# Last combination of a two-layer attention and expert kernel: three of eight batches on ScalarE and GpSimd

## Chip, cores and metric

The kernel runs on one core of one Trainium2 chip. The metric is the device time of one execution in microseconds; the median of several executions counts.

## What is computed

`x` is 8 batches of 256 tokens with 256 features, float32. Two layers follow each other. Each adds to `x` a gated cross-attention over 120 context rows, and then a gated mixture of 8 experts of which each token uses two. The end of a layer, cut to what matters here, is

```python
x = x + jnp.tanh(g_xattn[l]) * attention_l(_layernorm(x), ctx)
x = x + jnp.tanh(g_ffn[l]) * experts_l(_layernorm(x))
...
sel = jnp.take_along_axis(out_all, top_k_idx[:, :, None], axis=1)
out = jnp.sum(sel * router_probs[:, :, None], axis=1)
```

So for each token the outputs of its two experts are multiplied by the token's two weights (with tanh of the gate in them) and added to `x`. This weighted sum, for the second layer, is the combination that the change touches.

## The kernel before

The five engines run programs of their own and meet at semaphores (`wait_ge`, `then_inc`). All of `x` stays on the chip as `x_sb`, 128 partitions x 16 tiles x 256: batch b is the tiles 2b and 2b + 1.

In each layer the attention and the routing run over 16 tiles. During them GpSimd computes the layer norm's reciprocal deviations in tiny operations (L458 to L463) and scatters normalised tokens to a buffer in device memory, sorted by expert (L488); ScalarE applies the norm (L558, L601: 128x256, scale and bias read from the chip's memory). Then the experts run over 39 blocks of 128 tokens: SyncE loads a block (L374), TensorE multiplies (L1302, L1329), ScalarE and VectorE copy and activate, and GpSimd scatters each block's result to its tokens' rows of `ys_dram` (L494).

When all blocks are stored, SyncE (waiting at L391) issues eight loads, one for each batch, of 512 KB into `yg` (L393): `yg[:, b, t, k, :]` is the output of choice k for tile t of batch b. Load b counts up the semaphore `D_gl[b]`. The function `combine(L, b)` of VectorE (L744 to L754) waits for that load and then issues four instructions at L753, for k = 0, 1 and t = 0, 1:

```python
v.scalar_tensor_tensor(out=xt, in0=yg[:, b, t, k, :], scalar=wcomb[:, 2 * b + t, k:k + 1],
                       in1=xt, op0=ALU.mult, op1=ALU.add)
```

The second of a tile waits for the first (`d_c1`), and each second one counts up `d_comb`. The weights `wcomb` are computed on VectorE just before the expert blocks (L1005 to L1015, semaphore `C_v`). The combination of layer 0 is spread over the attention of layer 1 (the same L753, from 522 to 632 us); that of layer 1 stands at the very end of VectorE's program, batches 0 to 7 one after another. SyncE goes through the batches in the same order: it waits for `d_comb`, issues the store of batch b, 256 KB from `x_sb` to `out` (L399), and in the end waits for all stores (L401). Loads and stores are all issued from SyncE, on one hardware queue, the loads first. During this tail ScalarE, TensorE and GpSimd have nothing to do; ScalarE's last work is a copy at L678 at 807.5 us, GpSimd's the last scatter.

Of the kernel before, what the change touches and what calls it, by code (L numbers as in the profile page):

```python
# [19 lines left out]
ALU = mybir.AluOpType  # L20
ACT = mybir.ActivationFunctionType
# [12 lines left out]
def apart(eng, passed, *waits):  # L34


    for sem, v in waits:
        need(eng, sem, v)
    if any(not isinstance(v, int) for _, v in waits):
        eng.sem_inc(passed, 1)  # L40


def flamingo_kernel(nc, x, ctx_rows, mask, g_xattn, g_ffn, attn_w, attn_b, router_w, experts, out):
    NB, S, D = x.shape
# [5 lines left out]
    NT = NB * S // P  # L50
# [4 lines left out]
    TOPK = 2  # L55
# [15 lines left out]
    with es:  # L71
        def sb(name, shape, dt=F32):
            return es.enter_context(nc.sbuf_tensor(name, shape, dt))

        def sem(name):
            return es.enter_context(nc.semaphore(name))


        x_sb = sb("x_sb", [P, NT, D])
# [46 lines left out]
        yg = w_all[:, NE * EW[1]:NE * EW[1] + NB * QT * TOPK * D].rearrange("p (b t k d) -> p b t k d", b=NB, t=QT, k=TOPK)  # L126
# [43 lines left out]
        wcomb = sb("wcomb", [P, NT, TOPK])  # L170
# [33 lines left out]
        D_gl = [sem(f"results_loaded{b}") for b in range(NB)]  # L204
# [5 lines left out]
        C_v = sem("consts_vector")  # L210
# [32 lines left out]
        d_comb, d_c1 = (sem(n) for n in ("combined", "combine_step"))  # L243
# [6 lines left out]
        b_x, b_up, b_h, b_hT, b_y = (sem(n) for n in ("blkT_psum", "up_psum", "h_used", "hT_psum", "y_psum"))  # L250
        e_x, e_act, e_hT, e_hTv, e_y, e_h = (sem(n) for n in ("blkT_ready", "act_ready", "hT_ready_a", "hT_ready_v", "y_ready", "h_ready"))
        g_z = sem("zeros_ready")
        d_bo = sem("bias_rows_step")
        g_id = sem("token_numbers_ready")
        g_pass = sem("results_passed")
# [12 lines left out]
            return v_early[0:K, b, :, :, :] if b < 2 else v_late[0:K, b - 2, :, :, :]  # L268

        FILL_V = {0: 2, 1: 3, 4: 4, 5: 5, 6: 6, 7: 7}  # L270

        def at(u):
            return u // 2, u % 2 == 0, u // 2 + 1 < NB

        def run_blocks(eng, l, step):


            for j in range(U3 + 1):
                step(j, j % U3, (j - 1) // U3, j == 0, False)
            with eng.Fori(1, (MAX_BLOCKS - U3) // U3) as i:  # L280
                for u in range(U3):
                    step(U3 * i + (1 + u), (1 + u) % U3, i, False, False)
            for j in (MAX_BLOCKS - 2, MAX_BLOCKS - 1):
                step(j, j % U3, (j - 1) // U3, False, j == MAX_BLOCKS - 1)
# [26 lines left out]
        def _(sp):  # L311
# [83 lines left out]
                                     "(t p k) d -> p t (k d)", t=QT, k=TOPK)).then_inc(D_gl[b], 16)  # L395
            ov = out.rearrange("b (t p) d -> p b t d", p=P)
            for b in range(NB):
                sp.wait_ge(d_comb, NT + 2 * (b + 1))
                sp.dma_start(ov[:, b, :, :], x_sb[:, 2 * b:2 * b + 2, :]).then_inc(D_out[b % 2], 16)  # L399
            sp.wait_ge(D_out[0], 16 * NB // 2)  # L400
            sp.wait_ge(D_out[1], 16 * NB // 2)  # L401
# [3 lines left out]
        def _(g):  # L405
# [31 lines left out]
            def late_consts():  # L437

                g.memset(tri[:], 1.0).then_inc(C_g, 1)
                g.memset(lower[:], 1.0).then_inc(C_g, 1)  # L440
                g.wait_ge(C_g, 15)

                g.affine_select(out=tri[:], in_=tri[:], compare_op=ALU.is_ge, fill=0.0, base=-1,
                                pattern=[[1, P]], channel_multiplier=-1).then_inc(C_g, 1)

                g.affine_select(out=lower[:], in_=lower[:], compare_op=ALU.is_ge, fill=0.0, base=-1,
                                pattern=[[1, NE], [-1, NE]], channel_multiplier=0).then_inc(C_g, 1)
                ramp(iota8[:], NE, 1, 0, 0).then_inc(C_g, 1)
                ramp(eR[:], NE, REGION, 0, 0).then_inc(C_g, 1)
                ramp(thr[:], NT, P, 0, 0).then_inc(C_g, 1)  # L450
                ramp(jrow[:], MAX_BLOCKS, 1, 0, 0).then_inc(C_g, 1)
                ramp(tokid[:], NT, TOPK * P, 0, TOPK).then_inc(C_g, 1)
                ramp(spare[:], MAX_BLOCKS, P, NT * P * TOPK, 1).then_inc(C_g, 1)
                g.wait_ge(C_g, 23)
# [10 lines left out]
            def ln1_rstd(B):  # L465
                f = B % 2
                g.wait_ge(d_mv1, 2 * B + 2)
                need(g, a_xn1, B - 1)
                rstd((mv1[:, f, :, 0], mv1[:, f, :, 1]), ve1[:, f, :], rstd1[:, f, :], nm1[:, f, :], mhalf[:],
                     g_ve1, g_pw1, B + 1, g_rs1)  # L470

            def ln2_rstd(G):
                qt = G % 2
                g.wait_ge(d_mv2, G + 1)
                need(g, a_xn2, G - 1)
                rstd((mv2[:, qt, 0:1], mv2[:, qt, 1:2]), ve2[:, qt:qt + 1], rstd2[:, qt:qt + 1], nm2[:, qt:qt + 1],
                     mhalf[:, 0:1], g_ve2, g_pw2, G + 1, g_rs2)

            def scatter(B):
                l, b = B // NB, B % NB  # L480
                s = (NU * l + 2 * b) % 6
                g.wait_ge(d_e0, B + 1)
                g.tensor_copy(xn2[:, s:s + 2, D], tokid[:, 2 * b:2 * b + 2]).then_inc(g_id, 1)
                g.wait_ge(g_id, B + 1)
                g.wait_ge(d_slot, B + 1)
                for t in range(2):
                    for k in range(TOPK):
                        g.indirect_dma_start(xs_dram, bass.IndirectOffsetOnAxis(ap=slot_now[:, B % 2, t, k:k + 1], axis=0),  # L488
                                             xn2[:, s + t, :], None).then_inc(D_sc[B % 2], 16)

            def store_block(l, j, u):
                J = MAX_BLOCKS * l + j
                apart(g, g_pass, (e_y, J + 1), (d_dest, J + 1))
                g.indirect_dma_start(ys_dram, bass.IndirectOffsetOnAxis(ap=dest_i[:, u:u + 1], axis=0),  # L494
                                     y_sb[:, u, :], None).then_inc(D_y[u], 16)

            for l in range(2):
                if l == 1:
                    g.memset(v_late[:, :, :, 1, :], 1.0).then_inc(C_vz, 1)
                ln1_rstd(NB * l)  # L500
                ln1_rstd(NB * l + 1)
                if l == 0:
                    late_consts()
                for u in range(NU):
                    b, even, nxt = at(u)
                    B, G = NB * l + b, NU * l + u
                    if even:
                        if b >= 3:
                            scatter(B - 3)
                    elif b + 2 < NB:  # L510
                        ln1_rstd(B + 2)
                    if u > 0:
                        ln2_rstd(G - 1)
                scatter(NB * l + NB - 3)
                ln2_rstd(NU * l + NU - 1)
                for h in range(2):
                    g.wait_ge(p_pv[h], NU * (l + 1))
                g.memset(zrow, 0.0).then_inc(g_z, 1)
                g.wait_ge(g_z, 2 * l + 1)
                g.memset(zrow[:, D:D + 1], 1000000.0).then_inc(g_z, 1)  # L520
                scatter(NB * l + NB - 2)
                scatter(NB * l + NB - 1)
                for j in range(U3):
                    store_block(l, j, j)
                with g.Fori(1, MAX_BLOCKS // U3) as i:
                    for u in range(U3):
                        store_block(l, U3 * i + u, u)


        @block.scalar  # L530
        def _(a):
# [9 lines left out]
            for l in range(2):  # L541
# [136 lines left out]
                    a.copy(hT[:, 0:n, :], ps[:, 4, 0:n * P].rearrange("p (c n) -> p c n", c=n)).then_inc(e_hT, 1)  # L678
                run_blocks(a, l, blk)


        @block.vector
        def _(v):
# [47 lines left out]
            for l in range(2):  # L731
# [13 lines left out]
                def combine(L, b):  # L745

                    v.wait_ge(D_gl[b], 16 * (L + 1))
                    for k in range(TOPK):
                        for t in range(2):
                            if k:  # L750
                                v.wait_ge(d_c1, 2 * (NB * L + b) + t + 1)
                            xt = x_sb[:, 2 * b + t, :]
                            v.scalar_tensor_tensor(out=xt, in0=yg[:, b, t, k, :], scalar=wcomb[:, 2 * b + t, k:k + 1],  # L753
                                                   in1=xt, op0=ALU.mult, op1=ALU.add).then_inc(d_comb if k else d_c1, 1)  # L754
# [125 lines left out]
                for u in range(NU):  # L880
                    b, even, nxt = at(u)
# [17 lines left out]
                    divide(G)  # L899
                    if l == 0 and u in FILL_V:  # L900
                        values(B0 + FILL_V[u], 5)
                logits_copy(G0 + NU - 3, 5)
# [115 lines left out]
                run_blocks(v, l, blk)  # L1018

            for b in range(NB):  # L1020
                combine(1, b)


        @block.tensor
        def _(t):
            t.wait_ge(C_id, 2)

            for l in range(2):
# [178 lines left out]
                for u in range(NU):  # L1207
# [18 lines left out]
                    if l == 0 and u == 0:  # L1226
                        t.wait_ge(a_ctx, 4)
                        t.wait_ge(d_v, 2)
                    if l == 0 and u - 1 in FILL_V:
                        t.wait_ge(d_v, FILL_V[u - 1] + 1)  # L1230
                    if l == 0 and u - 1 in (2, 3):
# [22 lines left out]
                    if u >= 2:  # L1254
                        x2_t(G - 2)
                    if l == 0 and u in FILL_V:
                        v_proj(B0 + FILL_V[u], 5)
                    if l == 0 and u in (2, 3):
# [135 lines left out]
```

## Time and profile before

| | us |
|---|---|
| median of 3 runs | 833.12 |
| the three runs | 834.97, 833.12, 832.74 |
| the profiled execution, its own time | 834.21 |
| the profiled execution, span from first to last instruction | 832.4 |

The span leaves 1.8 us of the profiled execution's own time around it. The profile counts instructions by engine (PE is TensorE, PEld its weight loads, DVE is VectorE, ACT ScalarE, POOL GpSimd, SP SyncE; a q behind a name is that engine's queue of instructions or DMAs), by line of the kernel (L753 is line 753) and by shape. All times in it are microseconds from the span's start unless ns is said. In a row of a group, "busy, mean ns of one | idle" are the summed busy time, the mean duration, and the idle time of the engine just before. "To landing" of a DMA is from its issue to the last byte's arrival. The last 22 us of the span are the tail of which this case speaks.

### The profile page before, as it was taken

To read this page: it belongs to the slowest core of one execution; us is meant where nothing else is said; L and a number is where in the kernel's file an instruction comes from. 1 tells how busy PE (TensorE), PEld (TensorE's weight loads), DVE (VectorE), ACT (ScalarE), POOL (GpSimd) and SP (SyncE) were. 2 spreads that over 40 slices of the span, in tenths; PEclk is the share of its full clock that TensorE was granted. 3 is DMA by queue.
4 is the path that set the end of the run, shared out by engine and by line. 5 is a ranking of instruction groups with operands and counts; after the bars stand their busy time and mean duration, and the time that the engine had idled before them with its cause. 6 is when DMAs were issued, how large, how long until landed. Compare 5 with 4: busy or idle time off the path is not lost.

```text
span 832.4 us, 19644 instructions
## 1 busy us (share of the span) xinstructions
PE 713.5 (86%) x6306; PEld 538.1 (65%) x6307; DVE 412.3 (50%) x1352; ACT 259.6 (31%) x489; POOL 212.2 (25%) x384
## 2 busy tenths in 40 slices
PE   4899999618999999999999999589899834999980
PEld 3668778506777777777777776477777722666650
DVE  4667787632233322323332332458888752444446
ACT  3555565311111112111111212156555420222220
POOL 4023444540110101011010101112445460333330
PEclk9999999857999999999999999879999965999995
DMA  8044446635111111111110102300112212333328
GB/s 215 9 170 127 161 130 183 200 111 149 32 32 32 38 30 33 32 32 32 32 38 27 36 13 85 137 27 28 54 59 79 97 70 90 93 99 99 93 74 309
DMA packets 50831, 70.41 MB, mean 85 GB/s; under 512 B 7687, under 2 KB 38023, under 8 KB 50771
## 3 DMA queue, kind: packets, MB, share of 16 engines
q1 hardware_dynamic: 42380, 50.85, 20.3%
q0 software_dynamic: 6816, 18.69, 6.4%
q8 instruction: 40, 0.66, 0.3%
q10 hardware_dynamic: 1575, 0.05, 0.2%
q14 instruction: 20, 0.16, 0.1%
HBM read 46.55 MB, written 23.02 MB: 84 GB/s over the span
## 4 chain that ended last, share of the span: by engine, by line
PE 72%; DVE 13%; issue 6%; POOL 3%; ACT 2%; SPq 2%; DMA 2%; DVEq 0%; POOLq 0%; ACTq 0%
PE ps L1302 27%; PE ps L1329 17%; PE ps L1319 5%; PE ps L1123 4%; PE ps L1090 3%; DVE x_sb L753 2%; PE ps L1288 2%; PE ps L1095 2%; PE ps L1062 2%; PE ps L1136 2%; DVE m L768 2%; PE ps L1040 2%; PE ps L1079 2%; DVE ctx_q L777 2%; PE ps L1115 1%
## 5 line engine op out<-in xcount | busy, mean ns | idle before, releaser
L1302 PE MATMUL ps<-w_all,share 128*128 x780 | 236.0, 450 | 3.2 <-DVE share L993 1.6
L1302 PEld LDWEIGHTS ps<-w_all,share 128*128 128x128 f32 x780 | 144.9, 194 | 69.3 <-issue 13.5
L494 POOL DMA_INDIRECT ys_dram<-share,dest_i x78 | 75.1, 963 | 382.6 <-DVE share L1000 374.2
L1329 PE MATMUL ps<-w_all,share 112*128 (+1 forms) x624 | 149.9, 383 | 1.3 <-DVE share L983 0.7
L1329 PEld LDWEIGHTS ps<-w_all,share 112*128 112x128 f32 (+1 forms) x624 | 113.1, 191 | 16.0 <-issue 1.7
L968 DVE TENSOR_TENSOR share<-share,ps 128x344 f32<-128x344 f32 x78 | 40.0, 513 | 145.7 <-PE ps L1302 136.2
L678 ACT COPY share<-ps 128x512 f32<-128x512 f32 (+1 forms) x78 | 37.5, 480 | 200.7 <-PE ps L1319 200.7
L768 DVE TENSOR_REDUCE m<-ps 128x8 f32<-128x960 f32 x64 | 70.3, 1138 | 11.1 <-PE ps L1079 11.0
L670 ACT ACTIVATE share<-ps 128x344 f32<-128x344 f32 x78 | 35.8, 459 | 117.9 <-PE ps L1302 117.9
L488 POOL DMA_INDIRECT xs_dram<-xn,slot_now x64 | 64.7, 1011 | 21.3 <-issue 14.6
L1000 DVE COPY share<-ps 128x256 f32<-128x256 f32 x78 | 33.0, 423 | 72.7 <-PE ps L1329 72.7
L458 POOL TENSOR_SCALAR nm<-mv 128x1 f32<-128x1 f32 (+1 forms) x48 | 11.6, 241 | 182.5 <-DVE mv L802 122.0
L1288 PE MATMUL ps<-ident,share 128*128 128x128 f32 x156 | 31.1, 282 | 31.2 <-DMA share<-xs_dram 30.9
L1288 PEld LDWEIGHTS ps<-ident,share 128*128 128x128 f32 x156 | 21.4, 145 | 48.0 <-issue 36.0
L1319 PE MATMUL ps<-ident,share 128*128 128x128 f32 (+1 forms) x312 | 49.2, 280 | 1.3 <-DVE share L973 0.5
L1090 PE MATMUL ps<-q_flat,w_all 32*120 32x256 f32 x512 | 42.7, 399 | 8.2 <-DVE ctx_q L777 6.0
L1319 PEld LDWEIGHTS ps<-ident,share 128*128 128x128 f32 (+1 forms) x312 | 36.0, 141 | 18.0 <-DVE share L973 8.3
L591 ACT ACTIVATE share<-ps,mask_col 120x1024 f32<-120x1024 f32 x32 | 33.9, 1111 | 37.5 <-PE ps L1095 37.5
L973 DVE TENSOR_TENSOR share<-share 128x256 f32<-128x256 f32 x39 | 16.6, 426 | 57.7 <-ACT share L674 57.7
L1095 PEld LDWEIGHTS ps<-share,sel 32*120 32x120 f32 x1024 | 42.6, 187 | 1.8
L1095 PE MATMUL ps<-share,sel 32*120 32x128 f32 x1024 | 42.0, 277 | 0.0
L1079 PE MATMUL ps<-w_all,q_flat 32*128 32x120 f32 x1024 | 36.5, 280 | 4.0 <-ACT q_flat L573 2.9
(165 smaller groups left out, 949.0 us busy)
## 6 DMA issues: line engine op xcount, KB each, us to landing
share<-xs_dram SPq DMA_DIRECT2D x78, 129.0 KB, 2.1
w_all<-ys_dram SPq DMA_DIRECT2D x16, 512.0 KB, 7.2
w_all<-gate SPq DMA_DIRECT2D x8, 688.0 KB
w_all<-up SPq DMA_DIRECT2D x8, 688.0 KB
w_all<-down SPq DMA_DIRECT2D x8, 560.0 KB
w_all<-w SPq DMA_DIRECT2D x16, 256.0 KB
xs_dram<-share SPq DMA_DIRECT2D x17, 129.0 KB, 2.3
out<-x_sb SPq DMA_DIRECT2D x8, 256.0 KB, 5.1
```

Source lines behind the costliest of these rows:

```text
L488: g.indirect_dma_start(xs_dram, bass.IndirectOffsetOnAxis(ap=slot_now[:, B % 2, t, k:k + 1], axis=0), xn2[:, s + t, :], None).then_inc(D_s ...
L494: g.indirect_dma_start(ys_dram, bass.IndirectOffsetOnAxis(ap=dest_i[:, u:u + 1], axis=0), y_sb[:, u, :], None).then_inc(D_y[u], 16)
L678: a.copy(hT[:, 0:n, :], ps[:, 4, 0:n * P].rearrange("p (c n) -> p c n", c=n)).then_inc(e_hT, 1)
L768: v.tensor_reduce(m4[:, :].rearrange("p (g r) -> p g r", r=Q4)[:, 2 * h:2 * h + 2, 0:4], ps[:, 2 * h:2 * h + 2, 0:4 * K].rearrange("p g (j ...
L968: v.tensor_tensor(h_sb[:, 344 * q:344 * q + 344], act_sb[:, 344 * q:344 * q + 344], ps[:, 2 * q + 1, 0:344], ALU.mult).then_inc(e_h, 1)
L1079: i = t.matmul(ps[:, g, j * K:(j + 1) * K], qT[rows, f, j // 2, j % 2, qt * P:(qt + 1) * P], kT_all[rows, b, j // 2, :], start=(l == 1), s ...
L1090: t.matmul(ps[0:K, 4 + g, 2 * m * P:2 * (m + 1) * P].rearrange("p (e q) -> p e q", e=2), kT_all[rows, b, m, :], qT[rows, f, m, :, qt * P:( ...
L1095: i = t.matmul(ps[0:K, 4 + g, j * P:(j + 1) * P], sel[rows, j, :], mT[rows, :], start=False, stop=(j % 2 == 1))
L1288: i = t.transpose(ps[:, 7, k * P:(k + 1) * P], xg[:, u, k * P:(k + 1) * P], ident[:, :])
L1302: i = t.matmul(ps[:, bank, 0:w], xgT[:, k, :], w_all[:, bass.ds(off + (k * UPW[l] + col - EW[l]), w)], start=(k == 0), stop=(k == KT - 1))
L1319: i = t.transpose(ps[0:n, 4 + c // 4, (c % 4) * P:(c % 4 + 1) * P], h_sb[:, at_:at_ + n], ident[:, :])
L1329: i = t.matmul(ps[:, 6, 0:D], hT[0:r, c, :], w_all[0:r, bass.ds(off + (KT * UPW[l] + c * D - EW[l]), D)], start=(c == 0), stop=(c == KD[l] ...
```

## The change

The last combination of batches 1, 4 and 7 leaves VectorE. For each of them ScalarE waits for the load, and multiplies the four tiles of `yg` by their weights in place (an activation with Identity and the weight as scale); after both tiles of a k it counts up `a_w`. GpSimd, at the end of its program, waits for `a_w` and adds each product to `x_sb` with a `tensor_tensor`; the second of a tile waits for the first. VectorE combines batches 0, 2, 3, 5 and 6 as before. SyncE's loop over the stores stays in batch order, and waits for `g_comb` (GpSimd) or `d_comb` (VectorE) by batch. The combination of layer 0 isn't changed.

```diff
--- before.py
+++ after.py
@@ -250,6 +250,9 @@
         b_x, b_up, b_h, b_hT, b_y = (sem(n) for n in ("blkT_psum", "up_psum", "h_used", "hT_psum", "y_psum"))
         e_x, e_act, e_hT, e_hTv, e_y, e_h = (sem(n) for n in ("blkT_ready", "act_ready", "hT_ready_a", "hT_ready_v", "y_ready", "h_ready"))
         g_z = sem("zeros_ready")
+        g_c1 = sem("combine_step_pool")
+        a_w = sem("results_weighted")
+        g_comb = sem("combined_pool")
         d_bo = sem("bias_rows_step")
         g_id = sem("token_numbers_ready")
         g_pass = sem("results_passed")
@@ -268,6 +271,8 @@
             return v_early[0:K, b, :, :, :] if b < 2 else v_late[0:K, b - 2, :, :, :]
 
         FILL_V = {0: 2, 1: 3, 4: 4, 5: 5, 6: 6, 7: 7}
+
+        POOL_BATCHES = (1, 4, 7)
 
         def at(u):
             return u // 2, u % 2 == 0, u // 2 + 1 < NB
@@ -395,7 +400,10 @@
                                      "(t p k) d -> p t (k d)", t=QT, k=TOPK)).then_inc(D_gl[b], 16)
             ov = out.rearrange("b (t p) d -> p b t d", p=P)
             for b in range(NB):
-                sp.wait_ge(d_comb, NT + 2 * (b + 1))
+                if b in POOL_BATCHES:
+                    sp.wait_ge(g_comb, 2 * (POOL_BATCHES.index(b) + 1))
+                else:
+                    sp.wait_ge(d_comb, NT + 2 * len([n for n in range(b + 1) if n not in POOL_BATCHES]))
                 sp.dma_start(ov[:, b, :, :], x_sb[:, 2 * b:2 * b + 2, :]).then_inc(D_out[b % 2], 16)
             sp.wait_ge(D_out[0], 16 * NB // 2)
             sp.wait_ge(D_out[1], 16 * NB // 2)
@@ -525,6 +533,15 @@
                 with g.Fori(1, MAX_BLOCKS // U3) as i:
                     for u in range(U3):
                         store_block(l, U3 * i + u, u)
+
+            for n, b in enumerate(POOL_BATCHES):
+                for k in range(TOPK):
+                    g.wait_ge(a_w, 2 * n + k + 1)
+                    for t in range(2):
+                        if k:
+                            g.wait_ge(g_c1, 2 * n + t + 1)
+                        xt = x_sb[:, 2 * b + t, :]
+                        g.tensor_tensor(xt, xt, yg[:, b, t, k, :], ALU.add).then_inc(g_comb if k else g_c1, 1)
 
 
         @block.scalar
@@ -678,6 +695,14 @@
                     a.copy(hT[:, 0:n, :], ps[:, 4, 0:n * P].rearrange("p (c n) -> p c n", c=n)).then_inc(e_hT, 1)
                 run_blocks(a, l, blk)
 
+            a.wait_ge(C_v, 2 + 6 * 2)
+            for b in POOL_BATCHES:
+                a.wait_ge(D_gl[b], 32)
+                for k in range(TOPK):
+                    for t in range(2):
+                        i = a.activation(yg[:, b, t, k, :], yg[:, b, t, k, :], ACT.Identity, scale=wcomb[:, 2 * b + t, k:k + 1])
+                    i.then_inc(a_w, 1)
+
 
         @block.vector
         def _(v):
@@ -745,10 +770,11 @@
                 def combine(L, b):
 
                     v.wait_ge(D_gl[b], 16 * (L + 1))
+                    before = NB * L + (b if L == 0 else len([n for n in range(b) if n not in POOL_BATCHES]))
                     for k in range(TOPK):
                         for t in range(2):
                             if k:
-                                v.wait_ge(d_c1, 2 * (NB * L + b) + t + 1)
+                                v.wait_ge(d_c1, 2 * before + t + 1)
                             xt = x_sb[:, 2 * b + t, :]
                             v.scalar_tensor_tensor(out=xt, in0=yg[:, b, t, k, :], scalar=wcomb[:, 2 * b + t, k:k + 1],
                                                    in1=xt, op0=ALU.mult, op1=ALU.add).then_inc(d_comb if k else d_c1, 1)
@@ -1018,7 +1044,8 @@
                 run_blocks(v, l, blk)
 
             for b in range(NB):
-                combine(1, b)
+                if b not in POOL_BATCHES:
+                    combine(1, b)
 
 
         @block.tensor
```

## Rows read from the trace of the kernel before

**Rows 1.** The page, its first table: busy time and share of each engine
```profile
PE 713.5 (86%) x6306; PEld 538.1 (65%) x6307; DVE 412.3 (50%) x1352; ACT 259.6 (31%) x489; POOL 212.2 (25%) x384
```

**Rows 2.** The chain of waits, 780 to 833 us: start, duration, what
```profile
810.46 2.39 DMA ys_dram<-share,dest_i
...
812.92 4.09 DMA w_all<-ys_dram
...
817.04 12.36 DVE x_sb L753 x31
```

**Rows 3.** The timeline, 790 to 833 us: start, duration, engine, line, operation, count
```profile
812.92 4.27 SPq L393 DMA_DIRECT2D w_all<-ys_dram  x8
817.04 12.76 DVE L753 SCALAR_TENSOR_TENSOR x_sb<-w_all,wcomb,x_sb 128x256 f32<-128x256 f32 x32 [7.40 <-DMA w_all<-ys_dram]
818.74 11.46 SPq L399 DMA_DIRECT2D out<-x_sb  x8
```

**Rows 4.** L393, the loads 0 and 1, then 6 and 7: issue and landing
```profile
L393 SPq DMA_DIRECT2D w_all<-ys_dram x2: 387/425/463, 812.9 to 813.4; - x2
...
DMA to landing us min/median/max: 4.1/4.6/5.0
...
L393 SPq DMA_DIRECT2D w_all<-ys_dram x2: 472/522/572, 816.1 to 816.6; - x2
...
DMA to landing us min/median/max: 9.1/9.4/9.8
```

**Rows 5.** L399, the stores 0 and 7: issue and landing
```profile
L399 SPq DMA_DIRECT2D out<-x_sb x1: 383/383/383, 818.7 to 818.7; - x1
...
DMA to landing us min/median/max: 8.4/8.4/8.4
...
L399 SPq DMA_DIRECT2D out<-x_sb x1: 372/372/372, 829.8 to 829.8; - x1
...
DMA to landing us min/median/max: 2.1/2.1/2.1
```

**Rows 6.** Two stretches of the tail, and the queue's total from 805 us
```profile
core 0: us, PE busy (x) PEld busy (x) DVE busy (x) ACT busy (x) POOL busy (x), PEclk, DMA share, GB/s
817.00:820.00 3.00, 0.00 (x0) 0.00 (x0) 2.96 (x8) 0.00 (x0) 0.00 (x0) 0.50 1.04 398
...
826.00:829.00 3.00, 0.00 (x0) 0.00 (x0) 3.00 (x9) 0.00 (x0) 0.00 (x0) 0.50 1.09 383
...
q1 hardware_dynamic: 4352, 6.29, 62.7%
```

**Rows 7.** DMA rate in 40 slices of 0.175 us from 826 us
```profile
GB/s 386 375 386 375 404 380 380 381 386 386 380 381 375 398 380 392 386 375 380 386 380 386 386 375 345 287 182 304 334 357 351 123 0 0 0 0 0 0 0 0
```

**Rows 8.** ScalarE: groups by line and shape, and one pair in the timeline
```profile
L558 ACT ACTIVATE share<-x_sb,nm,rstd 128x256 f32<-128x256 f32 x32 | 17.5, 594 | 18.0 <-POOL nm L463 17.8
...
L558 ACT ACT_TABLE_LOAD x1 | 1.3, 1283 | 8.1 <-POOL nm L463 8.1
...
634.74 1.09 ACT L558 ACTIVATE share<-x_sb,nm,rstd 128x256 f32<-128x256 f32 x2 [1.13 <-POOL nm L463]
```

**Rows 9.** GpSimd: groups by line and shape
```profile
L463 POOL TENSOR_TENSOR nm<-nm,rstd 128x1 f32<-128x1 f32 x32 | 6.1, 192 | 2.5
...
L418 POOL TENSOR_SCALAR_AFFINE_SELECT sel<-sel 128x480 f32<-128x480 f32 x1 | 0.6, 600 | 0.0
...
L412 POOL TENSOR_SCALAR_AFFINE_SELECT ident<-ident 128x128 f32<-128x128 f32 x1 | 0.3, 285 | 0.1
```

**Rows 10.** The timeline of GpSimd near 581 and 676 us
```profile
581.16 0.45 POOL L458 TENSOR_SCALAR nm<-mv 128x1 f32<-128x1 f32 x1 [5.04 <-DVE mv L802]
581.69 0.31 POOL L459 TENSOR_SCALAR ve<-mv 128x1 f32<-128x1 f32 x1
...
675.91 0.24 POOL L458 TENSOR_SCALAR nm<-mv 128x1 f32<-128x1 f32 x1
```

**Rows 11.** The timeline of VectorE near 581 us
```profile
581.05 1.67 DVE L753 SCALAR_TENSOR_TENSOR x_sb<-w_all,wcomb,x_sb 128x256 f32<-128x256 f32 x4
```


## Prediction, made before the changed kernel ran

> **What bounds the kernel now.** The page's first table [rows 1] shows TensorE busy for 86% of the span, but the change touches only the end, so I read the end. The chain of waits [rows 2] says what the last 22 us consist of: the scatter of the last block (2.4 us), the load of the experts' results (4.1 us), then 12.4 us of VectorE's combination (L753). The timeline [rows 3] shows 32 combining instructions without a gap from 817.04 to 829.80, and the eight stores issued in between. On this reading VectorE bounds the tail, and taking 3 of 8 batches from it should give back up to 3/8 of 12.8 us = 4.8 us.
>
> The DMA rows contradict that. The first load lands at 812.9 + 4.1 = 817.0, the last at 816.6 + 9.8 = 826.4 [rows 4], one every (826.4 - 817.0)/7 = 1.34 us. Store 0 is issued at 818.7 and lands at 827.1, store 7 at 829.8 and 831.9 [rows 5]: stores leave VectorE (829.8 - 818.7)/7 = 1.59 us apart but land (831.9 - 827.1)/7 = 0.69 us apart. They queue behind the loads, and that queue is full: 398 GB/s from 817 to 820 and still 383 from 826 to 829, of 6.29 MB in all [rows 6]. Only around 830.5 does the rate dip (287 and 182 GB/s in slices of 0.175 us [rows 7]), some 0.3 us of missing bytes. So the floor of the DMAs lies about 0.3 us under today's end, and only the last store is tied to the arithmetic.
>
> A useful form of this: store b must be issued 2.1 us before its landing slot, by 825.0 + 0.69b; it is issued at 818.7 + 1.59b [rows 5]. Its slack is 6.3 - 0.9b: 5.4 us for batch 1, 2.7 for batch 4, none for batch 7. Batch 7 is one of the three that change engine.
>
> **The change part by part.** *VectorE* loses 12 instructions of 0.40 us pitch (12.76/32 [rows 3]). Since each remaining batch must land first, this brings batch 6, not the last one, forward: at best it lands at 816.1 + 9.1 = 825.2 [rows 4] and is combined at 826.8.
>
> *ScalarE* gets 12 multiplications of 128x256 in place. The nearest row is its layer-norm application, SBUF to SBUF with scale and bias from SBUF: 594 ns, two of them in 1.09 us [rows 8]; so 0.50 us pitch and 2.1 us a batch. It has stood idle since its last copy, and its wait on the weights of the combination was met when the expert blocks began. For batch 7: starts 826.45, first pair done 827.55, second 828.6. That alone is more than VectorE's four instructions of the batch (1.6 us). A table load costs 1.28 us [rows 8]; it occurs three times in all (at L558, L670 and L593), never for an Identity once a set is loaded, so I add none; on batch 1 it would be under 5.4 us of slack.
>
> *GpSimd* gets 12 additions of two 128x256 operands. No such row exists. Below: a one-column multiplication of two operands takes 192 ns; ends of 128 and 480 columns of the select give (600 - 285)/352 = 0.895 ns a column [rows 9]. If two operands cost no more than one, 192 + 255 x 0.895 = 420 ns. Above: if both reads and the write follow each other, 192 + 3 x 228 = 877 ns. I take two passes, 192 + 2 x 228 = 650 ns, because the nearest rows differ from this operation by one more operand to read. Free of others, consecutive ones start 0.08 us after the end of the one before (581.16 + 0.45 to 581.69 [rows 10]), which with the hand-over from ScalarE makes a pitch of about 0.77 us. GpSimd's own queue is empty then: its last scatter is issued at 810.46 [rows 2]. Alone, batch 7 would run 827.7 + 4 x 0.77 = 830.8, and its store would be issued 1.0 us later than now. With additions of 420 ns the end is set by ScalarE: 828.7 + 2 x 0.5 = 829.7, 0.1 us earlier than now.
>
> *Both on SBUF.* GpSimd's tiny operation on the layer-norm statistics takes 0.24 us when VectorE is quiet (675.91), but 0.45 us at 581.16, where combining instructions of VectorE run [rows 10, 11]. VectorE's instruction began at 581.05 and the next 0.40 later; GpSimd finished just after the changeover. So GpSimd waited for VectorE's instruction and not merely ran slowly beside it; I read off that a combining instruction keeps it out until 0.38 us after its start, holding for 0.28 of its 0.40 us. No row shows a long GpSimd operation, so whether VectorE waits in return is not visible. I take it that it does, since what keeps one out must be something both need, and charge 0.55 of the 0.65 us as holding time. The Trainium skill (SBUF — State Buffer, "SBUF: two separate sides") states this: the pair of ports that VectorE and GpSimd share is an exclusive lock for the whole instruction, for a VectorE instruction with two SBUF inputs against a GpSimd one that reads SBUF. It speaks against this change: by it the end comes as below, without it by the 1.0 us above. The trace agrees for one of the two directions.
>
> With it, one VectorE and one GpSimd instruction cost 0.28 + 0.55 = 0.83 us as a pair while both have work. Walked through: batch 1 lands at 818.4 [rows 4], its first products are there at 819.6, and its additions alternate with batch 2 from 819.85 to 819.85 + 4 x 0.83 = 823.2. Batch 3's first two go alone to 823.96. Batch 4's four additions, held up until then, alternate with the last two of batch 3 and the first of batch 5: 823.96 + 4 x 0.55 + 3 x 0.28 = 827.0. Batch 5's other three end at 828.1. Batch 7's additions, ready since 827.7, alternate with batch 6: 828.1 + 4 x 0.83 = 831.4. *SyncE* issues in batch order, so store 7 stands behind store 6: 831.5, and, as its issues are 0.5 us apart (eight in 4.27 us [rows 3]), 832.0. Today: 829.8. Stores 1 to 5 (issued at 823.0, 823.5, 825.7, 827.1, 828.2) meet their slots (825.7 to 828.5); only 6 and 7 miss them. The last store then needs its 2.1 us, as now.
>
> Sum: 832.0 - 829.8 = **+2.2 us**; the removed instructions of VectorE count for nothing, covered first by the landing of loads and then by the alternation. The profiled execution has a span of 832.4 us and took 834.21 us in all, which would become 836.4. The median of the three runs is 833.12, 1.1 us under it, so the forecast is 833.12 + 2.2 = **835.3 us**. A measurement can tell about 0.3%, 2.5 us.
>
> **Rivals.**
> *Slower by over 0.3%: the addition itself is longer.* Place: batch 7, after 828. Price: 12 additions stand in the alternation, so each 0.1 us more of holding adds about 1.2 us: holding for 0.65 us gives +3.4 us, 836.5; the upper bound of 0.77 gives +4.9, 838.0. It decides from about 0.57 us of holding on, 0.02 above my value. For it: my slope comes from one-input operations. Against: nothing direct. The Trainium skill (GPSIMD Engine Reference, "Performance versus the Vector engine") puts two-input elementwise work at about 2.6 cycles an element at 1.2 GHz; as an estimate, 192 + 255 x 2.17 = 745 ns and an end near 836.5. No run so far shows it.
>
> *VectorE does not wait for GpSimd.* Then batch 6 is done by 827 and batch 7 costs +1.0 us: 834.1 (up to +1.9 with the longest addition, 4 x 0.23 us more). For it: one direction only is in the trace. Against: the wait in rows 10.
>
> *Short additions.* One pass: -0.1 us, 833.0, with or without the lock, since ScalarE then sets the pace.
>
> *Faster by over 0.3%,* as the reading of the chain alone would have it (830.6 or less): the queue would have to carry the same 6.3 MB faster or start earlier, and the change moves no load. Rows 6 leave it 0.3 us.
>
> *That the change does nothing:* the work on the last batch is the longest chain of the three, so it must be seen.
>
> **How the numbers follow.** Forecast with the lock and +1.3 to +2.5 us: 0.38. Longer additions, over +2.5: 0.37. No waiting of VectorE, +0.3 to +1.3: 0.15. Short additions: 0.08. Faster: 0.02. This gives faster 0.02, same 0.61, slower 0.37. The range runs from the lower edge of the third case (833.3) to the upper bound of the addition (838.0).
>
> **What would show it.** GpSimd: 12 additions after 819, 0.65 us when alone, longer (up to 0.93) beside L753. VectorE: starts of its combining instructions stretched from 0.40 to 0.83 us where GpSimd runs; if they stay at 0.40, the lock is wrong. ScalarE: 12 of 0.6 us, the last ending near 828.6. The last store issued at about 832.0, landing 2.1 us later; landing of the loads unchanged to 0.1 us. I am wrong if batch 7's store is issued before 830, or if the end is set by something other than the last two stores.

## The result, and the profile after

| | before | after |
|---|---|---|
| median of 12 runs each | 834.62 us | 836.68 us |
| lowest and highest | 832.74, 835.65 | 834.33, 838.22 |
| the profiled execution, its own time | 834.21 | 836.53 |
| its span | 832.4 | 834.7 |

The ratio is 1.0028, with a 95% interval of 1.0017 to 1.0040: the changed kernel is slower by 1.4 to 3.3 us, 2.3 us in the middle. Timed again in a later session it was 1.0017 (1.0002 to 1.0033). Of the three runs of before that stood ahead of the prediction two, the middle one among them, lie below the median of its twelve.

The chain of waits of the changed kernel, from 810 to 835 us (start, duration, what), answers to [rows 2]:

```profile
810.40 2.40 DMA ys_dram<-share,dest_i
...
813.83 5.79 DMA w_all<-ys_dram
819.62 0.02 issue
819.64 11.32 DVE x_sb L779 x15
```

VectorE (its combining line is L779 now) has 20 instructions in place of 32, and the chain still runs through it for 11.3 us, against 12.4. The timeline of the same kernel, from 816 us, shows why; it answers to [rows 3]:

```profile
816.63 1.67 DVE L779 SCALAR_TENSOR_TENSOR x_sb<-w_all,wcomb,x_sb 128x256 f32<-128x256 f32 x4 [7.05 <-DMA w_all<-ys_dram]
818.02 1.70 ACT L703 ACTIVATE w_all<-w_all,wcomb 128x256 f32<-128x256 f32 x4 [10.17 <-DMA w_all<-ys_dram]
818.33 13.94 SPq L407 DMA_DIRECT2D out<-x_sb  x8
819.01 3.12 POOL L544 TENSOR_TENSOR x_sb<-x_sb,w_all 128x256 f32<-128x256 f32 x4 [7.65 <-ACT w_all L703]
819.64 11.71 DVE L779 SCALAR_TENSOR_TENSOR x_sb<-w_all,wcomb,x_sb 128x256 f32<-128x256 f32 x16 [1.34 <-DMA w_all<-ys_dram]
822.35 1.71 ACT L703 ACTIVATE w_all<-w_all,wcomb 128x256 f32<-128x256 f32 x4 [2.63 <-DMA w_all<-ys_dram]
823.34 3.44 POOL L544 TENSOR_TENSOR x_sb<-x_sb,w_all 128x256 f32<-128x256 f32 x4 [1.20 <-ACT w_all L703]
826.38 1.71 ACT L703 ACTIVATE w_all<-w_all,wcomb 128x256 f32<-128x256 f32 x4 [2.32 <-DMA w_all<-ys_dram]
827.37 3.31 POOL L544 TENSOR_TENSOR x_sb<-x_sb,w_all 128x256 f32<-128x256 f32 x4 [0.58 <-ACT w_all L703]
```

Sixteen combining instructions of VectorE take 11.71 us where sixteen took 6.4 before. They end at 831.4, one instruction after GpSimd's last addition (830.7). Durations by line (least, median, greatest, in ns) show both engines stretched; first GpSimd's additions, then three instructions of VectorE around 829 us:

```profile
L544 POOL TENSOR_TENSOR x_sb<-x_sb,w_all x12: 713/899/905, 819.0 to 829.8; 128x256 f32<-128x256 f32 x12
```

```profile
L779 DVE SCALAR_TENSOR_TENSOR x_sb<-w_all,wcomb,x_sb x3: 939/941/941, 828.3 to 830.0; 128x256 f32<-128x256 f32 x3
```

An addition takes 713 ns alone and 900 ns beside VectorE; a combining instruction takes 480 ns alone and 940 beside GpSimd. The three starts (828.29, 829.16, 830.02) are 0.87 us apart: one pair per 0.87 us. VectorE alone does two such instructions in 0.80 us. So taking an instruction from VectorE and giving its sum to GpSimd returns nothing while VectorE has work.

The ends of the tail, the last load (L398) and the last store (L407), with issue and landing, answer to [rows 4, 5]:

```profile
L398 SPq DMA_DIRECT2D w_all<-ys_dram x1: 594/594/594, 816.5 to 816.5; - x1
...
DMA to landing us min/median/max: 9.9/9.9/9.9
```

```profile
L407 SPq DMA_DIRECT2D out<-x_sb x1: 469/469/469, 831.8 to 831.8; - x1
...
DMA to landing us min/median/max: 2.5/2.5/2.5
```

The last load lands at 826.4, as before. The last store is issued at 831.8 and not 829.8 (+2.0 us), and needs 2.5 us and not 2.1, since the store of batch 6 was issued only 0.4 us ahead of it and its bytes go first (+0.3; in the runs below with batch 1 alone and with batches 0, 2 and 5, where the last two were 1.6 us apart and the loads long done, it was 2.1 again). These two terms are the 2.3 us by which the span grew.

From here on the tail is counted from the issue of its first load to the span's end: 19.5 us before (832.4 - 812.9), 21.9 after (834.7 - 812.9). Some experiments ran on other chips, where everything ahead of the tail took up to 40 us longer for every kernel; within the tail they agree. Where no time is given for an experiment, it had one execution, and only its trace is read.

### The profile page after: what moved, and what is told of

Its sections match the earlier page's. It is cut to its first block, busy times and chain, and to the rows that moved or that the text cites. A ratio compares the mean times of both kernels' runs of the same rounds, so it can differ in the third digit from the quotient of the medians.

```text
span 834.7 us, 19660 instructions
## 1 busy us (share of the span) xinstructions
PE 713.4 (85%) x6306; PEld 538.1 (64%) x6307; DVE 412.7 (49%) x1340; ACT 264.4 (32%) x501; POOL 221.5 (27%) x396
## 4 chain that ended last, share of the span: by engine, by line
PE 72%; DVE 13%; issue 6%; POOL 3%; DMA 2%; SPq 2%; ACT 2%; DVEq 0%; POOLq 0%; ACTq 0%
PE ps L1329 27%; PE ps L1356 16%; PE ps L1346 5%; PE ps L1150 4%; PE ps L1117 3%; PE ps L1122 2%; PE ps L1315 2%; DVE x_sb L779 2%; PE ps L1089 2%; PE ps L1163 2%; PE ps L1106 2%; PE ps L1067 2%; DVE m L794 2%; DVE ctx_q L803 1%; PE ps L1142 1%
## 5 line engine op out<-in xcount | busy, mean ns | idle before, releaser
L1329 PEld LDWEIGHTS ps<-w_all,share 128*128 128x128 f32 x780 | 144.7, 194 | 69.3 <-issue 13.5
L496 POOL DMA_INDIRECT xs_dram<-xn,slot_now x64 | 64.6, 1009 | 21.4 <-issue 14.6
L1315 PEld LDWEIGHTS ps<-ident,share 128*128 128x128 f32 x156 | 21.4, 145 | 48.2 <-issue 36.2
```

The costliest lines, as they stand in the source:

```text
L1315: i = t.transpose(ps[:, 7, k * P:(k + 1) * P], xg[:, u, k * P:(k + 1) * P], ident[:, :])
L1329: i = t.matmul(ps[:, bank, 0:w], xgT[:, k, :], w_all[:, bass.ds(off + (k * UPW[l] + col - EW[l]), w)], start=(k == 0), stop=(k == KT - 1))
```

## Experiments

The theory was that VectorE's combining instructions (two operands in SBUF) and GpSimd's additions exclude each other, in both directions, and that the last store is late by what this costs plus a small part for batch 7's own chain. The rivals were that any activity of GpSimd slows VectorE, that the chain through two engines costs by itself, and that VectorE bounded the tail before.

**GpSimd writes, but reads nothing.** Edit:

```diff
-                        g.tensor_tensor(xt, xt, yg[:, b, t, k, :], ALU.add).then_inc(g_comb if k else g_c1, 1)
+                        if n and not k:
+                            g.wait_ge(g_comb, 2 * n - 1 + t)
+                        g.memset(xn2[:, 3 * t:3 * t + 3, 0:D], 0.0).then_inc(g_comb if k else g_c1, 1)
```

> The changed kernel, but GpSimd's 12 additions are replaced by 12 fills of 128x768 of a scratch buffer (so the second half of batches 1, 4 and 7 isn't added): GpSimd is as long busy (its 128x768 fills took 0.73 to 0.75 us) but reads nothing from SBUF. Lock on what both read: VectorE's combining instructions keep their free pitch of 0.40 us beside GpSimd's, batch 6 is done about 1.6 us after its load, and only batch 7's chain on ScalarE and GpSimd is left: last store issued about 17.4 us after the first load's issue (16.9 before, 18.9 after). Rival, any work of GpSimd on SBUF holds VectorE up: pitch of 0.8 us or more, last store at 18.9 us or later.

VectorE's and GpSimd's groups in the tail:

```profile
L781 DVE SCALAR_TENSOR_TENSOR x_sb<-w_all,wcomb,x_sb x20: 476/478/486, 847.9 to 857.6; 128x256 f32<-128x256 f32 x20
```

```profile
L546 POOL MEMSET xn<- x12: 737/738/742, 850.2 to 860.5; 128x768 f32 x12
```

Nothing of the experts' results is added in batches 1, 4 and 7 here. GpSimd is busy as long per instruction as when it adds, and nobody is stretched. The last store was issued 17.3 us after the first load. The rival that any work of GpSimd slows VectorE falls.

**VectorE takes one of its two operands from PSUM.** Edit:

```diff
-                            v.scalar_tensor_tensor(out=xt, in0=yg[:, b, t, k, :], scalar=wcomb[:, 2 * b + t, k:k + 1],
+                            v.scalar_tensor_tensor(out=xt, in0=yg[:, b, t, k, :] if L == 0 else ps[:, 2 + t, 0:D],
+                                                   scalar=wcomb[:, 2 * b + t, k:k + 1],
```

> The changed kernel, but in the last combination VectorE takes the expert's results from PSUM (whatever lies there, so batches 0, 2, 3, 5, 6 come out differently) and so has one operand in SBUF where it had two; GpSimd's additions are as in the change. Lock only against two SBUF operands: VectorE's pitch 0.40, GpSimd's additions 0.71 us each as when alone, last store issued 17.2 us after the first load's issue. Rival, the engines slow each other whatever they read: pairs of 0.87 us, last store at 18.9 us.

The groups by line of the tail (busy, mean ns of one):

```profile
L544 POOL TENSOR_TENSOR x_sb<-x_sb,w_all 128x256 f32<-128x256 f32 x12 | 8.3, 723 | 10.7 <-ACT w_all L703 10.7
L779 DVE SCALAR_TENSOR_TENSOR x_sb<-ps,wcomb,x_sb 128x256 f32<-128x256 f32 x20 | 8.1, 476 | 9.5 <-DMA w_all<-ys_dram 9.5
```

GpSimd's real additions, 723 ns, beside VectorE's 476 ns: neither waits. The last store was issued at 17.6 us, a little over the 17.2 expected, because batch 7's load landed later in this run (ScalarE began it at 13.8 us in place of 13.5). So the exclusion needs both: GpSimd reading SBUF, and VectorE reading two operands from it. The Trainium skill (SBUF — State Buffer, "Who interferes with whom") says that a VectorE instruction with two inputs in SBUF contends with a GpSimd instruction that reads SBUF, and not with one that only writes it. These two runs agree. In the change both engines also read one tile, `w_all`, and in this run they don't; but in [rows 10] GpSimd waited while it read `mv`, which the combining instruction doesn't touch. So a common tile isn't needed for GpSimd to wait. For VectorE's waiting no run separates the two.

**ScalarE and GpSimd alone.** Edit:

```diff
-                    combine(1, b)
+                    pass
...
-                    sp.wait_ge(d_comb, NT + 2 * len([n for n in range(b + 1) if n not in POOL_BATCHES]))
+                    sp.wait_ge(D_gl[b], 32)
```

> The changed kernel without VectorE's last combination (batches 0, 2, 3, 5, 6 are stored without their experts' sum as soon as their load has landed): ScalarE and GpSimd alone. All 12 additions 0.71 us; batch 7: load at about 13.5 us after the first load's issue, products from 14.3, four additions at 0.68, last store issued at 17.2 us. So ScalarE's and GpSimd's chain alone costs about 0.3 us against before (16.9), and the rest of the change's 2.0 us is the mutual blocking. Rival, the batch's chain costs the most by itself: last store at 18.5 us or later with VectorE idle.

```profile
L544 POOL TENSOR_TENSOR x_sb<-x_sb,w_all x12: 713/722/726, 853.2 to 863.2; 128x256 f32<-128x256 f32 x12
```

The row is again GpSimd's additions by line. The last store was issued at 17.1 us: of the 2.0 us by which it is late in the change, 0.2 us are the chain of batch 7 and 1.8 us the exclusion (with the store of batch 6, which it holds up too). The split is only as good as the tail of before, whose last store left at 16.9 us in this trace and at 16.5 in the repetition below.

**Half of VectorE's work left out, in the kernel before.** Edit:

```diff
-                    for k in range(TOPK):
+                    for k in range(TOPK) if L == 0 else (1,):
                         for t in range(2):
-                            if k:
+                            if k and L == 0:
```

> The kernel before, but VectorE's last combination adds the second expert's results only (16 instructions in place of 32; the first expert's sum is left out), with the same loads and stores. Queue full: the last store lands 0.2 to 0.4 us earlier than before, 18.7 to 18.9 us after the first load's issue (before: 19.1). Rival, VectorE bounds the tail as the chain of waits says: the last store is issued 0.8 us after the last load and lands 2.1 us later, 16.4 us after the first load's issue.

The last load (L393) and the last store (L399), with issue and landing:

```profile
L393 SPq DMA_DIRECT2D w_all<-ys_dram x1: 546/546/546, 850.5 to 850.5; - x1
...
DMA to landing us min/median/max: 10.3/10.3/10.3
```

```profile
L399 SPq DMA_DIRECT2D out<-x_sb x1: 372/372/372, 861.7 to 861.7; - x1
...
DMA to landing us min/median/max: 4.5/4.5/4.5
```

With half the instructions the last store is issued 14.7 us after the first load (16.9 before), and then takes 4.5 us to land in place of 2.1: at 19.2 us, no earlier than before and later than the 18.7 to 18.9 expected. From the landing of the last load (850.5 + 10.3 = 860.8) to that of the last store it is 5.4 us; in the kernel before, 826.4 to 831.9, 5.5 us. The rival that the chain of waits suggested falls. The 0.3 us that the prediction still saw under today's end didn't show either, and the DMA rate tells what became of them (40 slices of 0.0675 us from 864 us):

```profile
GB/s 379 364 455 364 364 365 394 364 394 425 364 379 364 349 425 122 76 76 61 61 61 30 15 30 15 30 30 15 0 0 0 0 0 0 0 0 0 0 0 0
```

There is no dip, and the full rate ends at 865.0, 18.0 us after the first load's issue; in the kernel before it came back after the dip and held until 831.4 [rows 7], 18.5 us after it. But then the last bytes trickle for 0.9 us at 15 to 122 GB/s. One of the 16 DMA engines carries about 24 of the full 384 GB/s (an estimate, 384/16), so only a few of them still had work, and the last store lands only after they are done. Why they lag isn't shown. In the six tails of this case in which no addition of GpSimd held a store up, the last store landed 5.3 to 5.5 us after the last load, and the kernel before is the longest of them: at most 0.2 us could be had.

**A late fill by GpSimd, in the kernel before.** The first three runs brought something the prediction didn't have: with the last store issued at 17.1 to 17.6 us the span still ended at 21.0 to 21.4, 1.7 us after the last landing (0.5 in the kernel before). What ended last was GpSimd's closing entry, DRAIN at L71 (the `with` around the whole program). Edit, at the end of GpSimd's program:

```diff
+            g.wait_ge(d_comb, NT + 2 * NB)
+            g.memset(mhalf[:, 0:1], -0.5)
```

> The kernel before, with one fill of a single column at the end of GpSimd's program, after VectorE's last combination: no work to speak of, but GpSimd's last instruction is late. In the traces so far GpSimd's closing entry (L71) ends 3.6 us after its last instruction. If every program's closing has to be over before the kernel ends, the span ends about 17.0 + 0.2 + 3.6 + 0.4 = 21.2 us after the first load's issue, where it is 19.5 in the kernel before. Rival, the closing lies beside the stores and costs nothing: 19.5 us.

The entries of GpSimd at L71 in the last 4 us, and SyncE's wait for the last stores (L401):

```profile
L71 POOLq EVENT_SEMAPHORE  x2: 17/17/17, 868.2 to 868.2; - x2
...
L71 POOLq DRAIN  x1: 3714/3714/3714, 864.4 to 864.4; - x1
```

```profile
L401 SPq EVENT_SEMAPHORE  x1: 17/17/17, 866.8 to 866.8; - x1
```

A fill of 0.10 us at 864.42 keeps the kernel open until 864.4 + 3.7 = 868.1, though the stores had all landed at 866.8. The span ended 20.6 us after the first load's issue: 1.1 us more than before, 0.6 less than expected, since VectorE was through 0.4 us sooner than the 17.0 I had put in, and only 0.2 us followed the closing and not 0.4. The closing counts.

This also limits what the exclusion costs. It moved the stores by 1.8 us, but in the three runs without it the span was still 1.5 to 1.9 us longer than before, because GpSimd's closing then ended last. Of the 2.3 us of the change only 0.5 to 0.9 would come back if the engines didn't exclude each other.

**Batch 7 alone on ScalarE and GpSimd.** Edit: `POOL_BATCHES = (7,)`.

> The change with batch 7 alone moved: GpSimd meets VectorE only in the first two or three additions. Last store issued at 17.4 to 17.7 us after the first load's issue; GpSimd's last addition ends at 17.5 and its closing 3.6 us later, at 21.1. If the closing bounds the end, the span ends at 21.3 to 21.6; rival, the stores alone set the end: 20.0 to 20.3.

GpSimd's additions and closing, and SyncE's wait for the last stores (L409):

```profile
L544 POOL TENSOR_TENSOR x_sb<-x_sb,w_all x4: 716/717/964, 829.1 to 831.4; 128x256 f32<-128x256 f32 x4
```

```profile
L71 POOLq DRAIN  x1: 4932/4932/4932, 830.8 to 830.8; - x1
```

```profile
L409 SPq EVENT_SEMAPHORE  x1: 17/17/17, 834.3 to 834.3; - x1
```

Only one addition met VectorE (964 ns). The stores were in at 834.3, GpSimd's closing ended at 830.8 + 4.9 = 835.7, the span at 835.9: 21.3 us after the first load's issue, within the range for the closing and out of that for the stores.

**Batch 1 alone.** Edit: `POOL_BATCHES = (1,)`.

> The change with batch 1 alone moved. A pair of one VectorE and one GpSimd instruction took 0.87 us where VectorE alone does two in 0.80, and VectorE stands still until batch 2 lands; after that it has all of 2 to 7: last store issued 18.0 us after the first load's issue, span end about 20.6 (before 19.5, after 21.9); time against before 1.001. Rival, what is given to GpSimd early in the tail is free, since its store has 5 us of slack: last store at or below 16.9.

The timeline from the first addition on:

```profile
856.18 3.31 POOL L544 TENSOR_TENSOR x_sb<-x_sb,w_all 128x256 f32<-128x256 f32 x4 [7.65 <-ACT w_all L703]
856.52 11.17 DVE L779 SCALAR_TENSOR_TENSOR x_sb<-w_all,wcomb,x_sb 128x256 f32<-128x256 f32 x24 [1.06 <-DMA w_all<-ys_dram]
```

VectorE does 24 instructions in 11.17 us (9.6 without GpSimd). The last store was issued at 17.7 us (18.0 expected) and the span ended at 20.3. The direction is that of the theory, 0.8 us later than before, and the 5 us of slack of batch 1's own store didn't save it. Four instructions fewer save VectorE 1.6 us, but it stood still for 1.1 us until batch 2 had landed, and then lost 1.6 us in turns. The timing, 1.0004 (0.9989 to 1.0019), can't tell it from no change.

**Batches 0, 2 and 5.** Edit: `POOL_BATCHES = (0, 2, 5)`.

> The change with batches 0, 2 and 5 in place of 1, 4 and 7: as much work on GpSimd, but the last two batches are VectorE's and GpSimd is through by 15.7 us after the first load's issue, so its closing is over by 19.3. The alternation costs as before: last store issued at 18.8, span end 21.3 to 21.4, 0.5 us under the change; time against before 1.002. Rival, the choice of the last batch is what costs: last store at 16.9 to 17.2, span end 19.5 to 19.8, time as before.

```profile
852.35 6.77 POOL L544 TENSOR_TENSOR x_sb<-x_sb,w_all 128x256 f32<-128x256 f32 x8 [6.20 <-ACT w_all L703]
852.60 13.43 DVE L779 SCALAR_TENSOR_TENSOR x_sb<-w_all,wcomb,x_sb 128x256 f32<-128x256 f32 x20 [8.22 <-DMA w_all<-ys_dram]
```

In this timeline VectorE needs 13.43 us for 20 instructions where it needed 12.76 for 32. Last store issued at 18.4 us, span end at 21.0, both 0.3 to 0.4 us sooner than expected; time 1.0027 (1.0006 to 1.0048). With the last two batches on VectorE and GpSimd long done, most of the loss is still there: by these two traces the choice of batch 7 is worth about 0.9 us (21.9 to 21.0), the additions themselves about 1.5 (21.0 to 19.5), give or take the 0.4 us by which tails of one kernel differ. The times don't separate this kernel from the change.

**ScalarE weights, VectorE adds.** Edit, in VectorE's loop for batches 1, 4 and 7, with GpSimd's loop removed:

```diff
...
+                    continue
+                n = POOL_BATCHES.index(b)
+                for k in range(TOPK):
+                    v.wait_ge(a_w, 2 * n + k + 1)
+                    for t in range(2):
+                        if k:
+                            v.wait_ge(g_c1, 2 * n + t + 1)
+                        xt = x_sb[:, 2 * b + t, :]
+                        v.tensor_tensor(xt, xt, yg[:, b, t, k, :], ALU.add).then_inc(g_comb if k else g_c1, 1)
```

> ScalarE weights batches 1, 4 and 7 as in the change, but VectorE does their additions (tensor_tensor), in batch order; GpSimd does nothing. No second reader of SBUF beside VectorE: its combining instructions at 0.40 us, the additions a little under (128x256 of two SBUF operands took 426 ns against 480), last store issued 16.3 to 17.0 us after the first load's issue, span end 19.3 to 19.6: the change's whole loss is gone, and nothing is gained, since the queue of loads and stores is full. Rival, ScalarE's products on the last batch cost by themselves: last store at 17.5 or later.

One batch of the additions (L1049) and two of the old kind (L771) in the timeline:

```profile
863.23 1.42 DVE L1049 TENSOR_TENSOR x_sb<-x_sb,w_all 128x256 f32<-128x256 f32 x4
864.57 3.25 DVE L771 SCALAR_TENSOR_TENSOR x_sb<-w_all,wcomb,x_sb 128x256 f32<-128x256 f32 x8
```

Four additions take 1.42 us where four combining instructions take about 1.67, so VectorE has a little less to do; last store issued at 16.8 us, span end at 19.4. ScalarE's part of the change is harmless, and GpSimd's is the whole loss.

**The kernel before, once more, and the last store in halves.** Edit of the latter: batch 7 is combined tile by tile, and SyncE stores each tile by itself.

> The kernel before, unchanged, once more, for how far its tail varies by itself: first combining instruction 3.6 to 4.1 us after the first load's issue, last store issued 16.6 to 16.9, span end 19.4 to 19.6.

> The kernel before with the last batch finished tile by tile and stored in two halves of 128 KB, so that the queue has bytes to move in the gap that rows of before show near the end. Gain bounded by that gap: last landing 0.1 to 0.4 us earlier, span end 19.1 to 19.4; time against before 0.9995 to 1.0000, which this measurement can't tell from no change.

The kernel before ended at 19.1 us (831.0 - 811.9) here, 0.4 less than in the first profile and below the 19.4 to 19.6 expected: its loads had landed 0.4 us sooner (the first 3.7 us after its issue, against 4.1 in [rows 4]). So the tail of one kernel varies by 0.4 us. From the last load's landing to the last store's it was again 5.5 us. The kernel with the last store in halves ended at 19.1 too, time 1.0007 (0.9995 to 1.0018): nothing gained that can be measured.

**The change, once more.**

> The changed kernel, unchanged, once more and timed: last store issued 18.7 to 19.1 us after the first load's issue, span end 21.6 to 22.0, time against before 1.002 to 1.004.

Last store issued at 18.7 us, span end at 21.7 (835.2 - 813.5), time 1.0017 (1.0002 to 1.0033): the middle is just under what was expected, the tail within it. No kernel here beats the one before. The last store can't land sooner than the queue lets it, so no sharing of this arithmetic can gain more than the 0.2 us named above.

## Why the prediction was right

The forecast was +2.2 us, 835.3 us; measured were +2.3 us against the kernel before (ratio 1.0028), and a span longer by 2.3 us. The absolute median, 836.7, lies 1.4 us higher, because the kernel before, too, had a higher median over twelve runs than over the three I started from. That the two agree within 0.1 us is in part luck: the tail of one kernel varies by 0.4 us, and the errors below cancel. By its steps:

- *Not the chain of waits.* Right, and a little stronger than said: the floor lies at most 0.2 us under today's end and not 0.3. The missing bytes near 830.5 [rows 7] were hardly a gain to be had: with the last store issued 2.2 us earlier its landing was still 5.4 us after the last load's.
- *Both directions of the exclusion.* The trace of before had only GpSimd waiting for VectorE. VectorE waits in return (940 in place of 480 ns), and strictly in turns. The row at 581.16 was thin ground for it: the same line L458 ran five times beside combining instructions, and only at 566.1 and 581.2 it took longer (371 and 450 ns); the other three began within 0.02 us of the start of a combining instruction and took 238 to 242 ns, as when VectorE is quiet.
- *The addition.* Taken as 650 ns, measured 713 alone; the rival of a longer addition had its point of decision at 0.57 us of holding. The pair at 0.87 us less the prediction's 0.28 for VectorE gives 0.59 us, so that rival's condition was just met, and yet its result was not: the loss stayed under 2.5 us. The estimate worked out from the Trainium skill (GPSIMD Engine Reference, "Performance versus the Vector engine") was 745 ns, closer than mine. The pitch was too long, though: alone, additions followed each other after 0.68 us and not 0.77, each starting before the one ahead of it had ended. So batch 7 by itself costs its store 0.2 us (the run without VectorE), and not the 1.0 us that the prediction gave for it.
- *ScalarE.* Taken as 0.50 us from start to start; measured 0.40 (starts 818.02, 818.43, 818.83, 819.23), and no table load. Batch 1's load, too, landed 0.4 us sooner than in the trace of before, so its additions began at 819.0 and not 819.85, the first of them alone. Batch 7's second products were ready 0.5 us sooner, and its additions began at 827.4 and not 828.1. This offset the longer addition.
- *Walk and issue.* Store 7 was forecast at 832.0 and issued at 831.8, behind store 6 at 831.4, as said. Its landing was forecast at 2.1 us and took 2.5: the queue behind store 6 had been left out.
- *GpSimd's closing.* The step that is missing altogether. It ended at 829.0 + 5.3 = 834.3 in the changed kernel, in the same tenth of a microsecond as SyncE's wait for the last store:

```profile
L71 POOLq DRAIN  x1: 5297/5297/5297, 829.0 to 829.0; - x1
```

```profile
L409 SPq EVENT_SEMAPHORE  x1: 17/17/17, 834.3 to 834.3; - x1
```

Here it cost nothing beyond the stores, by chance: the span ended 0.4 us after the wait for the stores, as before, and after a closing that came last it is 0.2 us, so the closing had 0.2 us to spare. Without the exclusion the rival case, with its +1.0 us, would have been wrong by it: in the run with VectorE's operand in PSUM the last store was issued 0.7 us later than before, and the span ended 1.9 us later.

## What to carry to other kernels

Before an engine on the last link of the chain is relieved, look at the landing times on both sides of it: stores that leave 1.59 us apart and land 0.69 us apart are queued already, and half the arithmetic changed nothing. VectorE's instructions with two operands in SBUF and GpSimd's that read SBUF didn't run side by side here; they took turns, and a pair of turns (0.87 us) cost more than VectorE alone needed for both (0.80). If GpSimd is to help near the end, its last instruction should be over some 3.6 us before the stores are in.

## What the runs showed that was not expected

- GpSimd's closing (the DRAIN at L71) ended 3.6 us after its last instruction in every run: with a single-column fill (864.4 + 0.1 to 868.1), with additions (830.7 to 834.3 in the changed kernel), and in the kernel before, hidden, after its last scatter (810.4 + 4.6 = 815.0, from 811.4; the row below). The kernel doesn't end before it.

```profile
L71 POOLq DRAIN  x1: 4646/4646/4646, 810.4 to 810.4; - x1
```

- ScalarE's multiplication in place, SBUF to SBUF with only the scale read from SBUF, took 0.49 us at 0.40 us from start to start; its layer norm of the same shape, with scale and bias from SBUF, 0.59 and 0.50.
- The turns are fair: wherever both had such work, one instruction of each followed the other, and neither was kept out for a whole burst of the other's.
